# Product keys: two of every four weighings move from VectorE to GpSimd; the row-length count of two attentions goes through column tiles

## The chip, the cores and the metric

One core of one Trainium2 chip runs the whole program, a stack of four transformer layers in float32. The time is device microseconds (us) of one launch. The engines are PE (TensorE, matrix products), DVE (VectorE), ACT (ScalarE), POOL (GpSimd) and SP (which issues the transfers). Each runs its own list of instructions in order and waits on semaphores for the others.

## The reference

x has 16 batches of 128 tokens with 128 features. The change touches the third layer only (two attentions and a feed-forward with product keys):

```python
def self_attn(x, Wq, Wk, Wv):                       # cross_attn: the same without causal
    Q, K, V = (x @ Wq, x @ Wk, x @ Wv)
    energy = jnp.einsum('bqd,bkd->bqk', Q, K)
    lengths = jnp.sum(energy[:, 0] != 0, axis=-1)    # from the first query's row
    pad = kidx[None, None, :] >= lengths[:, None, None]
    energy = jnp.where(pad | causal, NEG_INF, energy)
    score = jax.nn.softmax(energy / np.sqrt(DK), axis=-1)
    return jnp.einsum('bqk,bkd->bqd', score, V)
...
def _L2_ffn_ref(x, w_q, keys, expert_down, expert_up, norm_w):   # H=8 heads, K=8, 32x32 experts
    sim1, sim2 = ...                                 # 32 similarities for either half of a key
    s1, i1 = top_k(sim1, K); s2, i2 = top_k(sim2, K)
    fs, pk = top_k(s1[..., :, None] + s2[..., None, :], K)
    hidden = gelu(einsum('btd,bthkd->bthk', xn, expert_down[fi])) * relu(fs)
    return einsum('bthk,bthkd->btd', hidden, expert_up[fi])
```

The kernel does not gather experts. It computes gelu(xn @ down) for all 1024 experts of each token, builds for each token a 32x32 table of given weights (the sum over heads of the scores that were chosen, zero elsewhere), multiplies the two element by element ("weighs") and projects out.

## The kernel before, in words

**Two attentions** (`two_attentions`). The 16 batches form four groups ("chunks", c = 0 to 3) of four. A list of stages (`ATTEND`), each one step later for each next group, gives one common order, `ORDER`, from which every engine takes its own instructions. Per group and attention: PE makes q, k (stage "project") and v ("values"), then in stage "scores" the scores, the causal part, and the counts: for each batch the product of all keys with the first query, 128 rows by 1 column. DVE turns these into 0 and 1 (`count`). Stage "length": PE adds them up over the rows with a column of ones, DVE copies the four lengths and makes a 4x128 row of large negative numbers (`measure_length`). Stage "mask": PE spreads it over the scores with four products. Then DVE takes row maxima ("top"), ACT the exponentials ("exp"), PE turns them ("flip"), ACT stores that, PE multiplies with v ("pv"), and layer norm and turning follow.

**Product keys** (`product_keys`). One round i for each batch i, and four rounds more to drain. In a round:

- PE: two chunks of the hidden layer of the next group of four (`hide`), the similarities of batch i+2 (`score`), the table of given weights of batch i-1 (`give`, 32 small products into the PSUM tile `given_ps`), and after the last batch of a group the projection (`project_out`, 128 products) and its turning (`finish`).
- DVE: maxima of the similarities of batch i (`tops`, 16 instructions), comparison against them (`parts`), the eighth best pair sum (`threshold`), the choice (`compare`, two instructions), the weighing of batch i-2 (`weigh`, hidden times `given_ps`, which it reads straight from PSUM), and two transposes of the factors (`turn`: right, then left).
- POOL: pair sums (two short ones), two sums of 512 elements into `factors`, and for the right and then the left side a subtraction and a product (`split_made`, `cut_made`), which `turn` waits for.
- ACT: a copy of half the similarities (`store_half`, which `tops` waits for), two gelus, and four copies that spread the turned right factor into `blocks` (`spread`, needs the right transpose and `given_made` of the batch before). `give` needs `blocks`, the left transpose, and the weighing of the batch before, since there is only one `given_ps`.

Of the kernel before, what the change touches and what calls it, by code (L numbers as in the profile page):

```python
# [15 lines left out]
P = 128  # L16
# [2074 lines left out]
def two_attentions(nc, m, w, tag, meanwhile, fold_of, keys_ahead, values_ahead):  # L2091
# [4 lines left out]
    ATTEND = ("project", "values", "scores", "length", "mask", "top", "exp", "flip", "pv", "stats", "scale", "turn")  # L2096
# [4 lines left out]
    with cleared_semaphores(nc) as new_semaphore, ExitStack() as ctx:  # L2101
# [12 lines left out]
        def room(n):  # L2114
# [10 lines left out]
        nonzero, length = chunk("nonzero", [P, 4]), chunk("length", [4, 1])  # L2125
        neg = chunk("neg", [4, S], BF16)
# [16 lines left out]
        nonzero_made, length_made, neg_made, neg_max_made = [  # L2143
            [sem(f"{n}{c}") for c in range(NCH)] for n in ("nonzero_made", "length_made", "neg_made", "neg_max_made")]
# [49 lines left out]
        def _(pe):  # L2194
# [22 lines left out]
            for name, a, c in ORDER:  # L2217
# [14 lines left out]
                elif name == "scores":  # L2232
                    work.wait_freed(pe, ("q", a, c), 0)
                    if not a:
                        work.wait_freed(pe, ("k", a, c), 0)
                    scores.wait_free(pe, (a, c), 0)
# [5 lines left out]
                    counts.wait_free(pe, (a, c), 0)  # L2242
                    for q in range(4):
                        ins = mm(counts.bank((a, c))[:, 0, q:q + 1], keys[a][c][:, q, :], qT[c][:, q, 0:1], start=True, stop=True)
                    counts.fill(ins, (a, c))
                elif name == "length":
                    pe.wait_ge(nonzero_made[c], a + 1)
                    mm(counts.bank((a, c))[0:4, 1, 0:1], nonzero[c][:, :], m["ones_sq"][:, 0:1],
                       start=True, stop=True).then_inc(length_made[c], 1)
                elif name == "mask":  # L2250
                    pe.wait_ge(neg_made[c], a + 1)
                    bank = scores.bank((a, c))
                    for q in range(4):
                        ins = mm(bank[:, q, :], m["pick_bf"][0:4, q, :], neg[c][:, :], start=False, stop=(q == 3))
                    scores.fill(ins, (a, c))
# [69 lines left out]
        def _(dve):  # L2325
# [3 lines left out]
            def count(a, c):  # L2329
                counts.wait_filled(dve, (a, c), 0)  # L2330
                V.tensor_scalar(nonzero[c][:, :], counts.bank((a, c))[:, 0, 0:4], 0.0, None, ALU.not_equal) \
                    .then_inc(nonzero_made[c], 1)

            def measure_length(a, c):
                dve.wait_ge(length_made[c], a + 1)
# [69 lines left out]
def product_keys(nc, m, w, tag, meanwhile):  # L2405
# [5 lines left out]
    with cleared_semaphores(nc) as new_semaphore, ExitStack() as ctx:  # L2411
# [81 lines left out]

        def exists(b):
            return 0 <= b < B

        @block.sync
        def _(sp):
            meanwhile(sp)
# [556 lines left out]
```

## Time and profile before

| | |
|---|---|
| runs, median (lowest to highest of 3) | 1214.05 us (1205.83 to 1220.04) |
| the profiled execution: its time | 1209.49 us |
| its span, first to last instruction | 1207.6 us |
| mean granted TensorE clock | 0.887 of full |
| PE, DVE, ACT, POOL busy over the span | 970.9, 744.0, 576.3, 391.7 us |
| the two attentions, 742.5 to 841 us of the span | 98.5 us |
| product keys, 841 to 1058.4 us | 217.4 us |

All positions below are microseconds from the start of the span. The busy shares over the whole span say little about either stage: they are an average over eight layers with different limits.

### The profile page before, as it was taken

The numbers are of one execution on the slowest core, as the hardware profiler recorded it, in microseconds if no ns is written. First come the engines' busy times: TensorE is split into PE (matmuls) and PEld (weight loads), VectorE is DVE, ScalarE is ACT, GpSimd is POOL, SyncE is SP. The second block draws the span as 40 slices with busy tenths as digits, with TensorE's granted clock in tenths as the row PEclk, the third lists the DMA queues.
The fourth block names the chain that finished last, engine by engine and source line by source line (L and its number), as shares of the span: only waits on it lengthen the run. The fifth ranks groups of instructions, "written<-read, shape, count | busy, mean of one in ns | idle before, by whom it ended". The sixth has DMA issues, their size and how long they took to land. (4 is left out here: it accounts for less than half of the span.)

```text
span 1207.6 us, 26748 instructions
## 1 busy us (share of the span) xinstructions
PE 970.9 (80%) x10817; PEld 642.7 (53%) x10845; DVE 744.0 (62%) x2025; ACT 576.3 (48%) x945; POOL 391.7 (32%) x418
## 2 busy tenths in 40 slices
PE   4999799998999977988897763785657577489987
PEld 2677333433333424776675562563456466447766
DVE  3586666546655464653574134468899999557752
ACT  3465465644555425644652631665535354235531
POOL 4320200000000022775002665146576656333340
PEclk9899799998999988998896886987878788789987
DMA  6000000000000016000000322000000000000000
GB/s 268 2 2 2 19 1 1 0 1 0 1 0 1 0 41 240 2 4 2 2 3 12 96 68 92 1 1 1 2 2 3 1 3 3 2 1 2 2 2 36
DMA packets 14713, 27.77 MB, mean 23 GB/s; under 512 B 1024, under 2 KB 12416, under 8 KB 13696
## 3 DMA queue, kind: packets, MB, share of 16 engines
q1 hardware_dynamic: 13568, 23.97, 5.5%
q0 software_dynamic: 1024, 2.10, 0.6%
q8 instruction: 87, 1.43, 0.5%
q14 instruction: 34, 0.28, 0.1%
HBM read 20.17 MB, written 5.90 MB: 22 GB/s over the span
## 5 line engine op out<-in xcount | busy, mean ns | idle before, releaser
L1324 PE MATMUL l0f_ctl<-l1f_in,l0f_in 128*128 128x512 f32 x320 | 145.7, 598 | 0.5
L548 DVE TENSOR_REDUCE l_neg_max<-l_ring 128x4 f32<-128x512 f32 x128 | 82.1, 684 | 63.5 <-PE l_ring L410 62.9
L128 POOL TENSOR_SCALAR row_var_eps<-row_mean_var 128x12 f32<-128x12 f32 (+2 forms) x16 | 3.7, 230 | 362.5 <-DVE row_mean_var L123 361.8
L2600 ACT COPY l2f_blocks_sb<-l2f_right_t_sb 32x1024 f32<-32x1024 f32 x64 | 66.8, 1043 | 86.6 <-PE l2f_given_ps L2531 75.5
L507 ACT ACTIVATE l_probs<-l_scores 128x1024 f32<-128x1024 f32 x64 | 65.6, 1025 | 82.2 <-PE l_scores L418 82.2
L1324 PEld LDWEIGHTS l0f_ctl<-l1f_in,l0f_in 128*128 128x128 f32 x320 | 61.7, 193 | 71.4 <-issue 70.2
L2531 PE MATMUL l2f_given_ps<-l2f_blocks_sb,l2f_left_t_sb 128*32 128x128 f32 x1024 | 50.1, 376 | 40.1 <-DVE l2f_hid_sb L2700 35.6
L2531 PEld LDWEIGHTS l2f_given_ps<-l2f_blocks_sb,l2f_left_t_sb 128*32 128x32 f32 x1024 | 44.0, 153 | 54.0 <-issue 53.8
L698 POOL TENSOR_TENSOR l_squares<-l_exps 128x1024 f32<-128x1024 f32 x32 | 60.6, 1895 | 29.8 <-ACT l_exps L953 29.8
L1045 DVE TENSOR_REDUCE l_neg_max<-l_scores 128x8 f32<-128x1024 f32 x32 | 39.2, 1225 | 43.4 <-PE l_scores L750 43.4
L368 POOL TENSOR_SCALAR_AFFINE_SELECT l_probs<-l_probs 128x1024 f32<-128x1024 f32 x32 | 35.0, 1094 | 64.0 <-ACT l_probs L507 64.0
L1597 DVE TENSOR_SCALAR l0f_halt<-l0f_halt 128x512 f32<-128x512 f32 x8 | 3.4, 427 | 78.8 <-ACT l0f_halt L1483 78.8
L1590 DVE SCALAR_TENSOR_TENSOR l1f_in<-l0f_index,l0f_in,l0f_hidden 128x512 f32<-128x512 bf16 x64 | 43.5, 747 | 12.2 <-ACT l0f_index L1464 11.0
L2664 POOL TENSOR_TENSOR l2f_factors_sb<-l2f_factors_sb,l1f_in 128x512 f32<-128x512 f32 x32 | 48.1, 1503 | 0.0
L953 ACT ACTIVATE l_exps<-l_scores 128x1024 f32<-128x1024 f32 x32 | 32.8, 1025 | 30.0 <-PE l_scores L756 29.8
L1324 PE MATMUL l0f_work<-xnT,l0f_in 128*128 128x512 f32 (+2 forms) x88 | 45.0, 683 | 1.3 <-ACT xnT L204 0.7
L750 PE MATMUL l_scores<-l_k_heads,l_q_all 32*128 32x256 f32 x256 | 36.8, 402 | 10.0 <-DVE l_neg_max L1045 8.3
L410 PE MATMUL l_ring<-l_k_heads,l_q_all 32*128 32x256 f32 x256 | 39.1, 424 | 6.5 <-ACT l_probs L507 2.4
L2509 PE MATMUL l2f_sim_ps<-l1f_in,xnT 128*128 128x512 f32 x32 | 22.5, 792 | 27.1 <-DVE l1f_in L2690 27.1
L1446 ACT ACTIVATE l0f_hidden<-l0f_work,l0f_in 128x512 f32<-128x512 f32 (+1 forms) x40 | 27.3, 686 | 29.0 <-PE l0f_work L1324 28.9
L992 ACT ACTIVATE l_exps<-l_scores 128x1024 f32<-128x1024 f32 x32 | 31.0, 1021 | 20.7 <-PE l_scores L837 20.7
L756 PE MATMUL l_scores<-l_q_all,l_k_heads 32*128 32x128 f32 x512 | 37.7, 286 | 1.8 <-ACT l_exps L953 1.8
(466 smaller groups left out, 2635.2 us busy)
## 6 DMA issues: line engine op xcount, KB each, us to landing
l1f_in<-in_l1f SPq DMA_DIRECT2D x1, 4580.0 KB, 13.5
l0f_in<-in_l0f SPq DMA_DIRECT2D x1, 2302.5 KB, 8.4
l1f_in<-in_l2u SPq DMA_DIRECT2D x1, 2048.0 KB, 8.7
sorted_rows<-first_in SPq DMA_DIRECT2D x1, 1856.0 KB, 10.4
l0f_in<-in_l2f SPq DMA_DIRECT2D x1, 1792.5 KB, 18.0
l1f_sorted<-sorted_rows SPq DMA_DIRECT2D x7, 256.0 KB, 4.9
expert_rows<-l1f_sorted SPq DMA_DIRECT2D x7, 256.0 KB, 2.2
x_in<-in_x SPq DMA_DIRECT2D x1, 1024.0 KB, 4.9
```

Of the source, the lines that this page charges most:

```text
L410: ins1 = mm(score_bank(b, half, g)[:, :, t, :], q_all[r, b, t, :], k_heads[r, b, t, :, :], start=not causal, stop=True, skip_group_check=True)
L507: nc.scalar.activation(probs[c % 2][:, 2 * pair:2 * pair + 2], scores2[:, :, :, :, :], ACT.Exp, scale=SCORE_SCALE).then_inc(exp_done, 1)
L548: ring.free(V.tensor_reduce(out, score_bank(b, half, g), AX.X, ALU.max, negate=True), ("score", b, half, g))
L698: nc.gpsimd.tensor_tensor(squares[c % 2][:, pair], e, e, ALU.mult).then_inc(squared, 1)
L750: ins1 = mm(scores1[:, g, :, t, :], q_all[r, b, t, :], k_heads[r, b, t, :, :], start=True, stop=True, skip_group_check=True)
L756: ins2 = mm(scores2[:, g, j, t, :], k_heads[r, c, t, j, :], q_all[r, c, t, :], start=True, stop=True, skip_group_check=True)
L1045: V.tensor_reduce(out, scores1[:, :, :, :, :].rearrange("p g j t s -> p (g j) t s"), AX.X, ALU.max, negate=True).then_inc(max_taken, 1)
L1324: return nc.tensor.matmul(out, lhs, rhs, start=start, stop=stop)
L1590: ins = STT(chosen[c % 2][:, k, p, :], index[k][:, c % 2, :], w["row_expert"][:, p:p + 1], hidden[c % 2][:, p, :], ALU.is_equal, ALU.mult)
L2531: ins = mm(given_ps[K * j:K * j + K, s, :, :], left_t[b % 2][:, 8 * j + s, :], blocks[:, 8 * j + s, :, :], start=True, stop=True)
L2600: A.copy(blocks[rows, :, u, :], right_t[rows, :, :]).then_inc(blocks_made, 1)
L2664: TT(value, value, kept[:, side, :, :], ALU.mult).then_inc(cut_made, 1)
```

## The change

**Product keys.** Of each four batches DVE weighs the first and the last, and POOL the second and third (`ON_POOL = (1, 2)`). POOL has no access to PSUM, so ACT first copies `given_ps` (128x1024) into `given_sb` (`store_given`, ahead of `spread` in the round), and `give` of the next batch waits for that copy and not for the weighing. POOL weighs at the end of its round and reads `given_sb` with its inner step over s, 128 elements apart. On DVE, the maxima of the next batch (`tops(i + 1)`) now stand ahead of the transposes of this one.

**Attentions.** The counts come first in stage "scores" and the other way round: the first 32 queries as weights and the keys as the moving side, so that batch q of the group writes rows 32q to 32q+31 of one PSUM tile, 128 columns wide. DVE compares with zero (128x128), sums along the row and makes a 128x512 mask that is -1 (never masked) outside each batch's own first row. PE adds that mask with one product. Stage "length" is gone, so "mask" and all behind it stand one step earlier in `ORDER`. Two constants move to the input group `l2f`, which grows by 288 KB, and one of 128 KB leaves the common group.

```diff
-    ATTEND = ("project", "values", "scores", "length", "mask", "top", "exp", "flip", "pv", "stats", "scale", "turn")
+    ATTEND = ("project", "values", "scores", "mask", "top", "exp", "flip", "pv", "stats", "scale", "turn")
...
+                    counts.wait_free(pe, (a, c), 0)
+                    for q in range(4):
+                        ins = mm(counts.bank((a, c))[32 * q:32 * q + 32, 0, :], qT[c][:, q, 0:32], keys[a][c][:, q, :],
+                                 start=True, stop=True)
+                    counts.fill(ins, (a, c))
                     scores.wait_free(pe, (a, c), 0)
...
-                    for q in range(4):
-                        ins = mm(counts.bank((a, c))[:, 0, q:q + 1], keys[a][c][:, q, :], qT[c][:, q, 0:1], start=True, stop=True)
-                    counts.fill(ins, (a, c))
-                elif name == "length":
-                    pe.wait_ge(nonzero_made[c], a + 1)
-                    mm(counts.bank((a, c))[0:4, 1, 0:1], nonzero[c][:, :], m["ones_sq"][:, 0:1],
-                       start=True, stop=True).then_inc(length_made[c], 1)
                 elif name == "mask":
                     pe.wait_ge(neg_made[c], a + 1)
-                    bank = scores.bank((a, c))
-                    for q in range(4):
-                        ins = mm(bank[:, q, :], m["pick_bf"][0:4, q, :], neg[c][:, :], start=False, stop=(q == 3))
-                    scores.fill(ins, (a, c))
+                    scores.fill(mm(scores.bank((a, c))[:, :, :], fold_of["first_rows_bf"][:, :], neg[c][:, :, :],
+                                   start=False, stop=True), (a, c))
...
+            def mask_beyond_length(a, c):
                 counts.wait_filled(dve, (a, c), 0)
+                counts.free(V.tensor_scalar(nonzero[c][:, :], counts.bank((a, c))[:, 0, :], 0.0, None, ALU.not_equal), (a, c))
                 counts.wait_freed(dve, (a, c), 0)
+                own(V.tensor_reduce(length[c][:, :], nonzero[c][:, :], AX.X, ALU.add))
+                V.tensor_scalar(neg[c][:, :, :], fold_of["key_of_row"][:, :, :], length[c][:, 0:1], NEG, ALU.is_ge, ALU.mult) \
                     .then_inc(neg_made[c], 1)
...
+    ON_POOL = (1, 2)
...
             def give(b):
                 pe.wait_ge(left_turned, b + 1)
                 pe.wait_ge(blocks_made, 4 * b + 4)
-                if b:
-                    pe.wait_ge(weighted, b)
+                if b and on_pool(b - 1):
+                    pe.wait_ge(given_stored, count(b, True))
+                elif b:
+                    pe.wait_ge(weighted, count(b, False))
...
+            def store_given(b):
+                act.wait_ge(given_made, b + 1)
+                if count(b, True):
+                    act.wait_ge(weighted_pool, count(b, True))
+                A.copy(given_sb[:, :, :, :], given_ps[:, :, :, :]).then_inc(given_stored, 1)
...
+                if exists(i - 2) and on_pool(i - 2):
+                    store_given(i - 2)
                 if exists(i):
                     spread(i)
...
+            def weigh(b):
+                g, q = b // GB, b % GB
+                if q == ON_POOL[0]:
+                    gelu_done(pool, b)
+                pool.wait_ge(given_stored, count(b + 1, True))
+                hidden = hid[g % 2][:, :, q, :].rearrange("p k (u s) -> p k u s", u=4)
+                TT(hidden, hidden, given_sb.rearrange("p s u k -> p k u s"), ALU.mult).then_inc(weighted_pool, 1)
...
+                if exists(b - 2) and on_pool(b - 2):
+                    weigh(b - 2)
+            weigh(B - 2)
...
             norm.dve(dve)
+            tops(0)
             for i in ROUNDS:
                 if exists(i):
-                    tops(i)
                     parts(i)
-                if exists(i):
                     threshold(i)
                     compare(i)
-                if exists(i - 2):
+                if exists(i - 2) and not on_pool(i - 2):
                     weigh(i - 2)
+                if exists(i + 1):
+                    tops(i + 1)
                 if exists(i):
                     turn(i)
```

DVE in product keys, one round before the change. MAX of 16 is `tops`, MAX of 8 `threshold`, the two TENSOR_TENSOR of 512 into `l1f_in` are `compare` (its tiles are carved from the space of `l1f_in`), the one on `l2f_hid_sb` is `weigh`:

```order
L2676 MAX l1f_in<-l2f_sim_ps 128x8 x16
L2686 TENSOR_TENSOR l2f_factors_sb<-l2f_sim_ps,l1f_in 128x8x64 x2
L2690 SCALAR_TENSOR_TENSOR l1f_in<-l2f_factors_sb,l2f_sim_ps 128x256
L2707 MAX l1f_in<-l1f_in 128x8 x8
L2715 TENSOR_TENSOR l1f_in<-l2f_factors_sb,l1f_in 128x512 x2
L2700 TENSOR_TENSOR l2f_hid_sb<-l2f_hid_sb,l2f_given_ps 128x32x32
L2723 STREAM_TRANSPOSE l2f_right_t_sb<-l2f_factors_sb 128x32x32
L2729 STREAM_TRANSPOSE l2f_left_t_sb<-l2f_factors_sb 128x32x32
```

The same place on DVE after the change, from `parts` of a round without a weighing to `tops` in the middle of it and the transposes:

```order
L2708 TENSOR_TENSOR l2f_factors_sb<-l2f_sim_ps,l1f_in 128x8x64 x2
L2712 SCALAR_TENSOR_TENSOR l1f_in<-l2f_factors_sb,l2f_sim_ps 128x256
L2728 MAX l1f_in<-l1f_in 128x8 x8
L2736 TENSOR_TENSOR l1f_in<-l2f_factors_sb,l1f_in 128x512 x2
L2698 MAX l1f_in<-l2f_sim_ps 128x8 x16
L2744 STREAM_TRANSPOSE l2f_right_t_sb<-l2f_factors_sb 128x32x32
L2750 STREAM_TRANSPOSE l2f_left_t_sb<-l2f_factors_sb 128x32x32
```

The weighing is gone from this round, and the 16 maxima stand where it stood, for the next batch.

POOL in the same rounds after the change (L2654 is the weighing, the only row that is new; the rest is a whole round of before between two weighings):

```order
L2654 TENSOR_TENSOR l2f_hid_sb<-l2f_hid_sb,l1f_in 128x32x32
L2663 TENSOR_TENSOR l1f_in<-l1f_in 128x8x16
L2666 TENSOR_TENSOR l1f_in<-l1f_in 128x8x12
L2672 TENSOR_TENSOR l2f_factors_sb<-l1f_in 128x8x64
L2675 TENSOR_TENSOR l2f_factors_sb<-l1f_in 128x8x64
L2680 TENSOR_TENSOR l2f_factors_sb<-l2f_factors_sb 128x8x32
L2683 TENSOR_TENSOR l2f_factors_sb<-l2f_factors_sb,l1f_in 128x8x64
L2680 TENSOR_TENSOR l2f_factors_sb<-l2f_factors_sb 128x8x32
L2683 TENSOR_TENSOR l2f_factors_sb<-l2f_factors_sb,l1f_in 128x8x64
L2654 TENSOR_TENSOR l2f_hid_sb<-l2f_hid_sb,l1f_in 128x32x32
```

The weighing ends POOL's round, so all that POOL does for the next batch stands behind it.

PE in the first attention before the change, one step of the order (L2201 the projections or, of 128x128, the values; L2239 scores; L2241 the causal part; L2244 counts; L2248 length; L2254 mask):

```order
L2201 MATMUL l_work<-xnT,l_in 128x512 x2
L2254 MATMUL l_scores<-l_neg_sb,common_in 128x128 x4
L2248 MATMUL l_counts<-common_in,l_nonzero_sb 4x1
L2239 MATMUL l_scores<-l_kT_sb,l_qT_sb 128x128 x4
L2241 MATMUL l_scores<-common_in 128x512
L2244 MATMUL l_counts<-l_qT_sb,l_kT_sb 128x1 x4
L2201 MATMUL l_work<-l_in,xnT 128x128 x4
```

The same step after it:

```order
L2200 MATMUL l_work<-xnT,l_in 128x512 x2
L2248 MATMUL l_scores<-l_neg_sb,l0f_in 128x512
L2237 MATMUL l_counts<-l_kT_sb,l_qT_sb 32x128 x4
L2243 MATMUL l_scores<-l_kT_sb,l_qT_sb 128x128 x4
L2245 MATMUL l_scores<-common_in 128x512
L2200 MATMUL l_work<-l_in,xnT 128x128 x4
```

The counts stand ahead of the scores, the length is gone, and the mask here is that of group 1 where before it was that of group 0.

## Rows read from the trace of the kernel before

**Rows 1.** Busy time of each engine in two stretches: attentions, then product keys.

```profile
core 0: us, PE busy (x) PEld busy (x) DVE busy (x) ACT busy (x) POOL busy (x), PEclk, DMA share, GB/s
742.50:841.00 98.50, 72.80 (x450) 54.69 (x452) 61.20 (x269) 57.62 (x157) 42.17 (x51) 0.86 0.06 22
841.00:1058.40 217.40, 142.12 (x3136) 117.37 (x3136) 194.94 (x561) 97.88 (x136) 128.68 (x136) 0.80 0.01 2
```

**Rows 2.** Timeline of DVE, one round of product keys: start, us, what.

```profile
908.92 1.29 DVE L2686 TENSOR_TENSOR l2f_factors_sb<-l2f_sim_ps,l1f_in 128x512 f32<-128x512 f32 x2
...
910.58 0.87 DVE L2707 MAX8 l1f_in<-l1f_in 128x8 f32<-128x36 f32 x8
911.49 1.99 DVE L2715 TENSOR_TENSOR l1f_in<-l2f_factors_sb,l1f_in 128x512 f32<-128x512 f32 x2
913.40 1.21 DVE L2700 TENSOR_TENSOR l2f_hid_sb<-l2f_hid_sb,l2f_given_ps 128x1024 f32<-128x1024 f32 x1
914.70 2.19 DVE L2723 STREAM_TRANSPOSE l2f_right_t_sb<-l2f_factors_sb 128x1024 f32<-128x1024 f32 x1
916.76 2.09 DVE L2729 STREAM_TRANSPOSE l2f_left_t_sb<-l2f_factors_sb 128x1024 f32<-128x1024 f32 x1
918.72 1.67 DVE L2676 MAX8 l1f_in<-l2f_sim_ps 128x8 f32<-128x32 f32 x16
920.41 1.29 DVE L2686 TENSOR_TENSOR l2f_factors_sb<-l2f_sim_ps,l1f_in 128x512 f32<-128x512 f32 x2
```

**Rows 3.** Timeline of DVE, first round: idle before it, and releaser, in brackets.

```profile
857.21 2.08 DVE L2723 STREAM_TRANSPOSE l2f_right_t_sb<-l2f_factors_sb 128x1024 f32<-128x1024 f32 x1 [1.25 <-POOL l2f_factors_sb L2664]
```

**Rows 4.** Timeline of POOL in the round of rows 2.

```profile
909.65 1.06 POOL L2653 TENSOR_TENSOR l2f_factors_sb<-l1f_in 128x512 f32<-128x512 f32 x1
910.75 1.06 POOL L2656 TENSOR_TENSOR l2f_factors_sb<-l1f_in 128x512 f32<-128x512 f32 x1
911.76 1.17 POOL L2661 TENSOR_TENSOR l2f_factors_sb<-l2f_factors_sb 128x256 f32<-128x256 f32 x1
912.89 1.71 POOL L2664 TENSOR_TENSOR l2f_factors_sb<-l2f_factors_sb,l1f_in 128x512 f32<-128x512 f32 x1
...
915.25 1.29 POOL L2664 TENSOR_TENSOR l2f_factors_sb<-l2f_factors_sb,l1f_in 128x512 f32<-128x512 f32 x1
```

**Rows 5.** Groups of instructions of 128x1024: busy, mean ns, idle before.

```profile
L507 ACT ACTIVATE l_probs<-l_scores 128x1024 f32<-128x1024 f32 x64 | 65.6, 1025 | 82.2 <-PE l_scores L418 82.2
L698 POOL TENSOR_TENSOR l_squares<-l_exps 128x1024 f32<-128x1024 f32 x32 | 60.6, 1895 | 29.8 <-ACT l_exps L953 29.8
```

**Rows 6.** Timeline at the end of product keys, ACT and PE.

```profile
1037.16 4.24 ACT L2600 COPY l2f_blocks_sb<-l2f_right_t_sb 32x1024 f32<-32x1024 f32 x4 [8.78 <-PE l2f_given_ps L2531]
...
1041.51 3.39 PE L2531 MATMUL l2f_given_ps<-l2f_blocks_sb,l2f_left_t_sb 128*32 128x128 f32 x64 [4.45 <-ACT l2f_blocks_sb L2600]
```

**Rows 7.** Timeline of PE in the first attention.

```profile
759.83 0.95 PE L2244 MATMUL l_counts<-l_qT_sb,l_kT_sb 128*128 128x1 f32 x8
760.64 1.14 PE L2201 MATMUL l_work<-l_in,xnT 128*128 128x128 f32 x8
...
764.86 0.39 PE L2254 MATMUL l_scores<-l_neg_sb,common_in 4*128 4x128 bf16 x4
765.18 0.19 PE L2248 MATMUL l_counts<-common_in,l_nonzero_sb 128*4 128x1 f32 x2
765.30 1.16 PE L2239 MATMUL l_scores<-l_kT_sb,l_qT_sb 128*128 128x128 f32 x8
```

**Rows 8.** Timeline of PE in product keys: products in column tiles.

```profile
926.06 1.95 PE L2520 MATMUL l2f_work_ps<-xnT,l0f_in 128*32 128x128 f32 x64 [0.34 <-ACT l1f_in L2608]
```

**Rows 9.** Timeline of ACT and DVE at the first exponentials of each attention.

```profile
768.50 0.59 ACT L2286 COPY l_v_sb<-l_work 128x512 f32<-128x512 f32 x1 [2.95 <-PE l_work L2201]
770.40 0.37 ACT L2301 ACTIVATE l_qT_sb<-l_scores,l_neg_max_sb 128x128 f32<-128x128 f32 x1
...
797.35 0.16 DVE L2331 TENSOR_SCALAR l_nonzero_sb<-l_counts 128x4 f32<-128x4 f32 x1 [1.42 <-PE l_counts L2244]
798.35 0.37 ACT L2301 ACTIVATE l_qT_sb<-l_scores,l_neg_max_sb 128x128 f32<-128x128 f32 x1 [2.74 <-DVE l_neg_max_sb L2344]
```

More of the change, by code:

```diff
@@ L2124, in two_attentions @@
         res = [[rows[:, 4 * c:4 * c + 4, :] for c in range(NCH)], room(0), room(1)]
-        nonzero, length = chunk("nonzero", [P, 4]), chunk("length", [4, 1])
-        neg = chunk("neg", [4, S], BF16)
+        nonzero, length = [room(1)[c][:, 0, :] for c in range(NCH)], chunk("length", [P, 1])
+        neg = chunk("neg", Q4, BF16)
         raw_max, neg_max = chunk("raw_max", [P, 4]), chunk("neg_max", [P, 4])
@@ L2142, in two_attentions @@
                        [sem("counts_filled")], [sem("counts_freed")])
-        nonzero_made, length_made, neg_made, neg_max_made = [
-            [sem(f"{n}{c}") for c in range(NCH)] for n in ("nonzero_made", "length_made", "neg_made", "neg_max_made")]
+        neg_made, neg_max_made = [[sem(f"{n}{c}") for c in range(NCH)] for n in ("neg_made", "neg_max_made")]
         eps_added, rstd_made, normed, res_made = [
@@ L2389, in _ @@
                 if name == "scores":
-                    count(a, c)
-                elif name == "length":
-                    measure_length(a, c)
+                    mask_beyond_length(a, c)
                 elif name == "top":
@@ L2495, in exists, with on_pool, count, gelu_done @@
             return 0 <= b < B
+        def on_pool(b):
+            return b % GB in ON_POOL
+        def count(b, pool):
+            return sum(on_pool(c) == pool for c in range(b))
+        def gelu_done(eng, b):
+            for c in range(KK - WORK, KK):
+                wait_freed(eng, ("hid", b // GB, c))
         @block.sync
@@ L2537, in project_out @@
                     wait_free(pe, ("out", g, j))
-                pe.wait_ge(weighted, GB * g + GB)
+                pe.wait_ge(weighted, count(GB * g + GB, False))
+                pe.wait_ge(weighted_pool, count(GB * g + GB, True))
                 for k in range(K):
@@ L2695, in weigh @@
                 if q == 0:
-                    for c in range(KK - WORK, KK):
-                        wait_freed(dve, ("hid", g, c))
+                    gelu_done(dve, b)
                 dve.wait_ge(given_made, b + 1)
```

18 lines of the change are left out of this document (7 added, 11 removed).

## The prediction

> **What bounds the kernel now.** The change lives in two stages, so I read the trace by stage first. In product keys DVE is busy 194.9 of 217.4 us, the others 60% or less [rows 1]; in the attentions no engine passes 75%, so order and latency set the time there and PE is merely the fullest.
>
> Then one round of product keys on DVE, by starts [rows 2]. From one `parts` (908.92) to the next (920.41) it takes 11.49 us: parts 1.66, threshold 0.91, compare 1.91, weigh 1.30, right transpose 2.06, left 1.96, maxima 1.69. There is no gap in it: what leaves DVE shortens the round, until another chain ends later. The nearest one is POOL's [rows 4]. Counted from the start of parts, its right product ends at 912.89 + 1.71 = 5.68 us and its left one at 915.25 + 1.29 = 7.62 us, and the two transposes start at 5.78 and 7.84. POOL is 0.1 us from being the bound. In the first round, which has nothing to weigh yet, it is: DVE stands idle for 1.25 us ahead of the right transpose, released by POOL's product [rows 3]; the second round, also without a weighing, looks the same. Taking the weighing away alone would thus turn 1.2 of its 1.3 us into a wait.
>
> **Product keys, DVE.** With the maxima of the next batch between compare and the transposes, the right transpose of a round without a weighing starts at 1.66 + 0.91 + 1.91 + 1.69 = 6.17 us (POOL is ready at 5.68), the left one at 8.23 (ready at 7.62), and the round ends at 10.19 instead of 11.49. POOL's chain hangs on `parts`, not on where the maxima stand, so its 5.68 and 7.62 hold: its second sum started at 1.83, behind parts, and does so still. The rounds that lose DVE's weighing and lie on the path are i = 3, 4, 7, 8, 11, 12 and 15 (batches 1, 2, 5, 6, 9, 10, 13; batch 14 falls in the drain). Six give 1.30 us each, 7.8. Round 15 has no maxima behind it and runs into POOL's 5.68 again: 0.1. Rounds 0 and 1 lose their wait: 2 x 1.2 = 2.4. Against this, rounds 8 and 12 follow a projection, for which PE holds back `give`, hence ACT's spreading and the copy that the maxima need, and the maxima now want it 3.5 to 4.8 us earlier in the round; following the chain with the durations of these rows I find some 0.5 us of wait in either, 1.1 together. Sum: 7.8 + 0.1 + 2.4 - 1.1 = 9.2 us. In the rounds with a weighing nothing is gained: their DVE work stays 11.49.
>
> **ACT's new copy.** Eight of 128x1024 from PSUM; the nearest row is 1.03 us [rows 5]. ACT is busy 97.9 of 217 us [rows 1], and the copy stands ahead of the spreading. What is queued behind it is the spreading of this round, which waits for the right transpose anyway, so seven of the eight lie in idle time. The last does not: behind the spreading of batch 15 (1037.16, 4.24 us) ACT now copies the table of batch 14 before the last `give` (1041.51) can start [rows 6]: +1.0. But the 8.78 us for which ACT waited there went on the `give` that DVE's weighing of batch 13 held up; it is now held by a copy that is done much earlier, and the spreading can start at the end of the right transpose, an estimated 1.7 us sooner. I book the end at 0 (bounds -0.7 and +1.0).
>
> **POOL's weighing, the unknown.** No row shows POOL on 1024 elements with a far inner step. Without the step: 1.9 us [rows 5], or twice 1.06 to 1.29 for 512, 2.1 to 2.6 [rows 4]; beside DVE's compare, which reads two SBUF tensors too, 512 took 1.71 and 256 took 1.17, hence 3.4 and 4.7. It starts at 7.62 and runs beside DVE's maxima and transposes, where the rows read 1.29, so I take 2.6. It ends at 10.2, the two short pair sums end 0.73 later at 10.95, and the next round's first sum of 1.06 ends at 12.0 = 10.19 + 1.8, just when the second sum could start. It costs nothing up to about 3.2 us, since the transposes leave another 0.5. From there I let each step of the two chains start at the later of its predecessors, round by round: 3.6 us leaves 7.9 of the 9.2 to 9.5, 4.4 leaves 4.7, 5.2 nothing, 6.5 makes it 10.6 us slower. Rounds behind an `add` or with a weighing on DVE absorb part of the delay, which is why the loss starts gently. For contention with two engines busier I take 0.2 off: 9.0 us.
>
> The Trainium skill speaks against my 2.6. "GPSIMD Engine Reference", section 7 (Performance pitfalls for Q7 kernels), says that a GpSimd read of SBUF whose step times element size is over 8 bytes costs about 50% more per element. Here the inner step of the given table is 128 elements. By it 2.6 would be 3.9 us, and the stage would give 6.7 instead of 9.0. No row of this trace shows such a read on POOL.
>
> **Attentions.** From the counts to the next product took PE 760.64 - 759.83 = 0.81 us, the length 765.30 - 765.18 = 0.12, the mask 0.32 [rows 7]. In column tiles 64 passes of 128 columns take 1.95 us [rows 8], so the eight of the new counts take 0.25. The one mask product writes the same 512 columns as the four: I take the same 0.32 (not below 0.2). Per group 0.56 + 0.12 = 0.68 us leave PE. In the first attention PE runs nearly without a gap up to the values of group 3; ACT stores these at 768.50, loads a table, and starts the first exponential at 770.40 [rows 9]. Ahead of them stand three counts and two lengths less, and one mask more: 1.7 + 0.2 - 0.3 = 1.6 us, which shift all that follows. In the second, the first exponential (798.35) waited 2.74 us for DVE, whose maxima stood behind the count of group 2 (797.35). Without the length stage they stand behind that of group 1, about 3.3 us earlier. Then the turning of the first probabilities is next, on PE behind the scores of group 3, with four counts and three to four lengths less ahead: 2.3 us after small waits. Together 3.9. The bounds are 1.5 (the waits eat the second) and 6. DVE's part grows from three short ones (0.57) to a compare of 128, a sum and a mask of 512, by estimate 1.0 us a group: between counts and mask PE has scores and a projection or values, over 2 us, and DVE is idle there. The 288 KB in the input load lie in a transfer that has a whole layer of cover; removed 128 KB at the start I count at nothing.
>
> **Sum.** 9.0 + 3.9 = 12.9 us. The profiled execution took 1209.49 us with a span of 1207.6, so its like would be 1196.6. It is 4.6 us under the median of the runs; against the median of 1214.05 I predict **1201 us**. A measurement of this kernel tells about 1% (12 us) from no change, and the forecast lies right at that edge.
>
> **Rivals.**
>
> 1. *The strided read costs POOL.* Weighing of 3.6 to 4.4 us, from the rows of 2.6 and the contended 4.7. Speaks for it: the inner step, and the rule above. Against: POOL's other reads here with hops between runs of 32 are not slow. Stage gain 4.7 to 7.9, total 10: 1204. Chance 0.2.
> 2. *The attentions give nothing*: the mask waits for DVE's longer work, or layer norm behind them is bound by DVE anyway. Total 9: 1205. Chance 0.1.
> 3. *POOL becomes the bound.* Strided and contended together: 3.4 us times 1.5 to 2, 5.1 to 6.8. `threshold` then waits for the pair sums and both transposes for the products, in all seven rounds; slower than before from 5.2 us in the stage and about 5.8 in the kernel; at 6.5, 10.6 - 3.9 = +6.7: 1221. Chance 0.05.
> 4. *More than summed*, as PE, with less to do, passes the slow stretches faster and the attentions give 6: total 16, 1198. Chance 0.1.
>
> **How the numbers follow.** The forecast has 0.55; its own spread (10.5 to 15) lies more than half beyond 12 us. Faster by over 1%: 0.34 of it, 0.08 of rival 4, 0.06 of 1 and 2 (the median of before is itself loose, 1206 to 1220), and 0.02 else: 0.50. Slower by over 1%: 0.03. The rest, 0.47, is within. Range: 1191 (a gain of 16 on a median 7 lower) to 1210.
>
> **What would show it.** In the profile after: rounds of product keys of 10.2 and 11.5 us by turns in pairs; POOL's weighing near 2.6 us, ending before the next parts start; no idle ahead of the right transposes but in round 15; on PE counts of 0.25 us and a first exponential 1.6, then 3.9 us earlier. I am wrong if the weighing takes over 3.3 us, if DVE waits for the copy of similarities, or if the mask product waits for DVE.

## The result, and the profile after

The changed kernel takes 1196.43 us (median of 20 runs, 1192.27 to 1207.09), the kernel before 1209.42 (20 runs, 1204.48 to 1220.04): a ratio of 0.9894, 95% interval 0.9874 to 0.9914, 13.0 us less. In a second session the ratio was 0.9869 [0.9837, 0.9901]. The forecast of 1201 us hung on a median of 1214.05 for the kernel before, of three runs; over twenty it is 1209.42, and the 4.6 us between them are the 4.6 by which 1201 was too high. Both ratios say a little over 1% faster, and both intervals reach to just under 1%: that the gain exceeds 1% is likely, not settled. The page of the profiled execution begins:

```profile
span 1191.8 us, 26693 instructions
...
PE 957.7 (80%) x10775; PEld 629.2 (53%) x10805; DVE 740.1 (62%) x2017; ACT 583.4 (49%) x953; POOL 414.4 (35%) x426
```

Where the time went is read by stage, from the first row of the layer norm on DVE in one stage to the first in the next:

| us | before | after | predicted |
|---|---|---|---|
| two attentions | 98.63 | 94.26 | -3.9 |
| product keys | 217.29 | 207.29 | -9.0 |
| all else, by the spans | 891.68 | 890.25 | 0 |

The last line is of layers that the change doesn't touch (more on it under the whole runs, below). The first two are of one execution each; in the others with the same code product keys took 206.8 to 207.0 us, and the attentions 94.2 or 95.4 (point 7 of the account of the prediction). The windows of the two stages answer to [rows 1]: DVE is busy 185.05 us in place of 194.94 in product keys, POOL 151.14 in place of 128.68.

```profile
core 0: us, PE busy (x) PEld busy (x) DVE busy (x) ACT busy (x) POOL busy (x), PEclk, DMA share, GB/s
742.70:836.90 94.20, 65.72 (x408) 45.48 (x412) 67.25 (x269) 57.68 (x157) 42.34 (x52) 0.90 0.06 23
836.90:1044.20 207.30, 136.59 (x3136) 113.22 (x3136) 185.05 (x553) 105.36 (x144) 151.14 (x145) 0.82 0.01 2
```

A round of product keys without a weighing on DVE, and the start of the next, which has one (compare [rows 2]; columns are start, us, engine, what):

```profile
889.63 1.29 DVE L2708 TENSOR_TENSOR l2f_factors_sb<-l2f_sim_ps,l1f_in 128x512 f32<-128x512 f32 x2
...
892.20 1.99 DVE L2736 TENSOR_TENSOR l1f_in<-l2f_factors_sb,l1f_in 128x512 f32<-128x512 f32 x2
894.12 1.65 DVE L2698 MAX8 l1f_in<-l2f_sim_ps 128x8 f32<-128x32 f32 x16
895.69 2.15 DVE L2744 STREAM_TRANSPOSE l2f_right_t_sb<-l2f_factors_sb 128x1024 f32<-128x1024 f32 x1
897.68 2.24 DVE L2750 STREAM_TRANSPOSE l2f_left_t_sb<-l2f_factors_sb 128x1024 f32<-128x1024 f32 x1
900.05 1.29 DVE L2708 TENSOR_TENSOR l2f_factors_sb<-l2f_sim_ps,l1f_in 128x512 f32<-128x512 f32 x2
...
902.62 1.99 DVE L2736 TENSOR_TENSOR l1f_in<-l2f_factors_sb,l1f_in 128x512 f32<-128x512 f32 x2
904.53 1.21 DVE L2721 TENSOR_TENSOR l2f_hid_sb<-l2f_hid_sb,l2f_given_ps 128x1024 f32<-128x1024 f32 x1
905.66 1.65 DVE L2698 MAX8 l1f_in<-l2f_sim_ps 128x8 f32<-128x32 f32 x16
```

From parts to parts it is 900.05 - 889.63 = 10.42 us, no idle in it. Behind the first maxima of the stage, the one wait for the copy of half the similarities is in round 7:

```profile
927.84 1.67 DVE L2698 MAX8 l1f_in<-l2f_sim_ps 128x8 f32<-128x32 f32 x16 [0.38 <-ACT l1f_in L2593]
```

POOL's weighing and ACT's copy of the table, as groups (count, then busy and mean ns, then the idle before):

```profile
L2654 POOL TENSOR_TENSOR l2f_hid_sb<-l2f_hid_sb,l1f_in 128x1024 f32<-128x1024 f32 x8 | 23.1, 2893 | 2.8 <-ACT l1f_in L2609 2.8
L2609 ACT COPY l1f_in<-l2f_given_ps 128x1024 f32<-128x1024 f32 x8 | 8.2, 1026 | 0.1
```

The last round and the drain on DVE: the right transpose waits again [rows 3], the last weighing waits for PE's `give`.

```profile
1019.28 2.08 DVE L2744 STREAM_TRANSPOSE l2f_right_t_sb<-l2f_factors_sb 128x1024 f32<-128x1024 f32 x1 [1.23 <-issue]
...
1030.52 1.22 DVE L2721 TENSOR_TENSOR l2f_hid_sb<-l2f_hid_sb,l2f_given_ps 128x1024 f32<-128x1024 f32 x1 [5.29 <-PE l2f_given_ps L2533]
```

In the first attention PE now goes from mask to counts to scores in 0.31 + 0.35 us (compare [rows 7]), and the first exponentials of the two attentions on ACT start 26.26 and 51.11 us after the stage's start, in place of 27.86 and 55.81 [rows 9]:

```profile
764.06 0.38 PE L2248 MATMUL l_scores<-l_neg_sb,l0f_in 128*128 128x512 bf16 x1
764.37 0.43 PE L2237 MATMUL l_counts<-l_kT_sb,l_qT_sb 128*32 128x128 f32 x8
764.72 1.16 PE L2243 MATMUL l_scores<-l_kT_sb,l_qT_sb 128*128 128x128 f32 x8
```

```profile
768.92 0.37 ACT L2295 ACTIVATE l_qT_sb<-l_scores,l_neg_max_sb 128x128 f32<-128x128 f32 x1
...
793.77 0.37 ACT L2295 ACTIVATE l_qT_sb<-l_scores,l_neg_max_sb 128x128 f32<-128x128 f32 x1
```

### The profile page after: what moved, and what is told of

Read it like the earlier page. It is cut to its first block and busy times, and to the rows that moved or that the text cites. A ratio compares the mean times of both kernels' runs of the same rounds, so it can differ in the third digit from the quotient of the medians.

```text
span 1191.8 us, 26693 instructions
## 1 busy us (share of the span) xinstructions
PE 957.7 (80%) x10775; PEld 629.2 (53%) x10805; DVE 740.1 (62%) x2017; ACT 583.4 (49%) x953; POOL 414.4 (35%) x426
## 2 busy tenths in 40 slices
DMA packets 14713, 27.94 MB, mean 23 GB/s; under 512 B 1024, under 2 KB 12416, under 8 KB 13696
## 3 DMA queue, kind: packets, MB, share of 16 engines
q0 software_dynamic: 1024, 2.10, 0.6%
```

## The experiments

Stage times below are read as in the table above. The kernels are named by what they are.

**One half of the change alone: `attn_only` and `keys_only`.** The changed kernel with `product_keys` of before, and the kernel before with `product_keys` of the changed one.

> The attentions of the changed kernel with the product keys of before. My theory (PE loses 0.68 us a group in the first attention, and in the second DVE's maxima stand one group earlier): the attentions end 3.9 us sooner (bounds 1.5 and 6), product keys take their old 217.3 us; against before -3.9 us, ratio 0.997. The rival that the attentions give nothing expects 0. A third reading, that the whole gain of 13 us has its source here, expects -13.

> The product keys of the changed kernel with the attentions of before. My theory: -9 to -10 us against before (ratio 0.992), all of it between the first normalising row of the layer and the first of the next, which goes from 217.3 to about 207.3 us. If the two parts help each other (the clock, for example) this and the attentions alone sum to less than 13; if they are independent, to 13 to 14.

| | attentions | product keys | run, median | ratio to before |
|---|---|---|---|---|
| attn_only | 94.22 | 217.25 | 1205.24 | 0.9957 [0.9929, 0.9986] |
| keys_only | 98.63 | 206.76 | 1206.59 | 0.9969 [0.9942, 0.9997] |

Each half works in its own stage, 4.4 and 10.5 us (in the whole kernel 4.4 and 10.0), and gives nothing in the other: the two parts don't interact inside the stages. The runs of `keys_only`, though, fell by 3.9 us only. That was taken up again (last experiment).

**The two moves in product keys apart: `maxima_only` and `weigh_only`**, both with the attentions of the changed kernel.

```diff
 # maxima_only: maxima ahead of the turns, all sixteen weighings on DVE
-    ON_POOL = (1, 2)
+    ON_POOL = ()
```

```diff
 # weigh_only: weighings split, each batch's maxima ahead of its own parts as before
-            tops(0)
...
+                    tops(i)
                     parts(i)
...
-                if exists(i + 1):
-                    tops(i + 1)
```

> The changed kernel, but DVE weighs all batches again; the next maxima stay ahead of the transposes. My theory: only the waits of rounds 0 and 1 go, 1.2 us each, so product keys take 217.3 - 2.4 = 214.9 us, and all later rounds 11.49 us. The rival that POOL's chain is shortened in every round by the early maxima expects rounds below 11.49 us.

> The changed kernel, but the maxima stand at the head of each round as before; POOL weighs two of four. My theory: in the rounds without a weighing DVE waits some 1.2 us for POOL's product ahead of the right transpose, so that seven weighings of 1.3 us buy about 0.1 us each: product keys take 216.3 us (-1). The rival that the DVE work removed is what counts (the order of the maxima being a detail) expects 217.3 - 9.1 = 208.2 us.

`weigh_only`: 217.36 us for the stage, no gain at all, where 1.0 us was expected. A round whose weighing had moved to POOL, on DVE:

```profile
891.54 1.99 DVE L2736 TENSOR_TENSOR l1f_in<-l2f_factors_sb,l1f_in 128x512 f32<-128x512 f32 x2
894.75 2.23 DVE L2744 STREAM_TRANSPOSE l2f_right_t_sb<-l2f_factors_sb 128x1024 f32<-128x1024 f32 x1 [1.23 <-issue]
896.89 2.06 DVE L2750 STREAM_TRANSPOSE l2f_left_t_sb<-l2f_factors_sb 128x1024 f32<-128x1024 f32 x1
898.86 1.22 DVE L2698 MAX8 l1f_in<-l2f_sim_ps 128x8 f32<-128x32 f32 x12
```

Between compare, which ends at 891.54 + 1.99, and the right transpose stand 1.2 us of idle in place of the weighing. The releaser is given as issue, but POOL's right product ended just before, at 892.94 + 1.72 = 894.66, and the gap is that of [rows 3] to 0.03 us. The 1.30 us that the weighing left are taken by POOL's chain, as worked out from [rows 4].

`maxima_only`: 213.68 us, 3.6 less, where 2.4 was expected. Its first round, with the maxima in the gap:

```profile
852.76 2.00 DVE L2734 TENSOR_TENSOR l1f_in<-l2f_factors_sb,l1f_in 128x512 f32<-128x512 f32 x2
854.69 1.65 DVE L2696 MAX8 l1f_in<-l2f_sim_ps 128x8 f32<-128x32 f32 x16
856.26 2.04 DVE L2742 STREAM_TRANSPOSE l2f_right_t_sb<-l2f_factors_sb 128x1024 f32<-128x1024 f32 x1
858.22 1.96 DVE L2748 STREAM_TRANSPOSE l2f_left_t_sb<-l2f_factors_sb 128x1024 f32<-128x1024 f32 x1
860.31 1.29 DVE L2706 TENSOR_TENSOR l2f_factors_sb<-l2f_sim_ps,l1f_in 128x512 f32<-128x512 f32 x2
```

No idle is left; the first two rounds are 1.24 and 1.21 us shorter than before. The other 1.2 us come from the later rounds, which take between 0.13 us more and 0.33 us less than before, half of it in rounds 7 and 11 (0.33 and 0.30); points 1 and 3 below show how the same instructions start sooner or later by their neighbours. So the moves are worth 3.6 and 0 us alone and 10.0 together: the weighing pays only once the maxima fill the gap.

**What the step in POOL's read costs: `dense_table`.**

```diff
-        given_sb = carve([8, 4, K])
+        given_sb = carve([K, 4, 8])
...
-                A.copy(given_sb[:, :, :, :], given_ps[:, :, :, :])
+                A.copy(given_sb.rearrange("p k u s -> p s u k"), given_ps[:, :, :, :])
...
-                TT(hidden, hidden, given_sb.rearrange("p s u k -> p k u s"), ALU.mult)
+                TT(hidden, hidden, given_sb[:, :, :, :], ALU.mult)
```

> The changed kernel with one thing other: ACT writes the given table into SBUF in the order in which POOL reads it, so that POOL's weighing reads runs without a gap in place of an inner step of 128 elements; ACT's copy now writes in short hops. The step is what it costs (rival 1 of the prediction, in a milder form): the weighing falls from the 2.90 us of the changed kernel to 2.1 to 2.6. The step costs nothing: it stays at 2.9. ACT's copy: 1.03 us or somewhat more. Either way the stage takes the 207.3 us of the changed kernel within 0.5, since POOL's chain has slack at 2.9 us.

```profile
L2654 POOL TENSOR_TENSOR l2f_hid_sb<-l2f_hid_sb,l1f_in 128x1024 f32<-128x1024 f32 x8 | 19.1, 2386 | 4.4 <-ACT l1f_in L2609 4.4
L2609 ACT COPY l1f_in<-l2f_given_ps 128x1024 f32<-128x1024 f32 x8 | 15.5, 1940 | 0.1
```

POOL falls from 2.89 to 2.39 us, ACT's copy grows from 1.03 to 1.94. The step was in POOL's price, 0.50 us or 21%, and moving it to ACT costs 0.91 there. The stage took 207.43 us. Both are slack in the rounds; the drain, where the copy stands in the chain, grew from 30.71 (after the last parts) to 31.65.

**How much slack POOL has: `pool_plus_512` and `pool_twice`.** Ahead of each of the eight weighings POOL does more work into a table that nothing reads (`spent` makes the engine wait for the end of each such instruction).

```diff
 # pool_plus_512
+                spent(TT(unused[:, :, :, :], given_sb[:, 0:4], given_sb[:, 4:8], ALU.mult))
                 TT(hidden, hidden, given_sb.rearrange("p s u k -> p k u s"), ALU.mult).then_inc(weighted_pool, 1)
```

```diff
 # pool_twice
+                for half in range(2):
+                    spent(TT(unused.rearrange("p s u k -> p k u s"), hidden[:, :, :, 0:4],
+                             given_sb[:, 4 * half:4 * half + 4].rearrange("p s u k -> p k u s"), ALU.mult))
```

> The changed kernel with one more product of 512 elements (contiguous, into a table that nothing reads) on POOL ahead of each of the eight weighings, so that POOL's work per weighing grows from 2.90 us to 4.1 to 4.4. The prediction's two chains then give a stage 3.5 to 5 us longer than the changed kernel's 207.3: 210.8 to 212.3, with DVE idle ahead of the threshold or the right transpose of the round behind each weighing. Rival: POOL's slack is larger than the 0.5 us that the prediction gave it, and the stage stays at 207.3 to 208.5.

> The changed kernel with POOL's strided product done once more (in two halves, into a table that nothing reads) ahead of each of the eight weighings: 5.8 to 6.2 us per weighing, the case of the prediction's rival 3. The two chains give a stage that is slower than that of the kernel before (217.3): 5 to 8 us slower, 222 to 225, or 15 to 18 above the changed kernel's 207.3. Rival: rounds with no weighing on POOL absorb more than the chains say, and the stage ends at 212 to 217.

With 1.28 us more per weighing the stage took 211.65 us, within what the two chains say. DVE now stands still for POOL ahead of the threshold and ahead of compare:

```profile
887.36 0.88 DVE L2732 MAX8 l1f_in<-l1f_in 128x8 f32<-128x36 f32 x8 [0.34 <-POOL l1f_in L2670]
888.45 2.61 DVE L2740 TENSOR_TENSOR l1f_in<-l2f_factors_sb,l1f_in 128x512 f32<-128x512 f32 x2 [0.21 <-POOL l2f_factors_sb L2676]
...
899.03 0.88 DVE L2732 MAX8 l1f_in<-l1f_in 128x8 f32<-128x36 f32 x8 [0.38 <-POOL l1f_in L2670]
900.11 2.58 DVE L2740 TENSOR_TENSOR l1f_in<-l2f_factors_sb,l1f_in 128x512 f32<-128x512 f32 x2 [0.21 <-POOL l2f_factors_sb L2676]
```

The waits are 0.34 and 0.21 us in the first such round, 0.38 and 0.21 in the next, and compare takes 2.6 us in place of 1.99. Four rounds (4, 5, 9 and 13) are 1.2 to 1.3 us longer for it. In the changed kernel the pair sums end 0.9 us ahead of the threshold (890.37 and 891.29 in the round shown above), and POOL's right product 0.35 ahead of its transpose. Yet the transposes don't wait here, since the threshold and compare, which come first, have been put off already. With 3.1 us more (two of 1.555) the stage took 226.70 us, 9.4 slower than the kernel before, and beyond the upper end of the expectation by 1.7:

```profile
892.91 0.88 DVE L2734 MAX8 l1f_in<-l1f_in 128x8 f32<-128x36 f32 x8 [2.36 <-POOL l1f_in L2672]
...
906.40 0.88 DVE L2734 MAX8 l1f_in<-l1f_in 128x8 f32<-128x36 f32 x8 [2.56 <-POOL l1f_in L2672]
```

Rival 3 of the prediction is thus real at a weighing of 6 us, twice the one that came, through the threshold; the transposes don't wait here either. The rounds account for 5.4 of the 9.4 us (181.60 against 176.20 in the kernel before, first to last parts). The drain gives the other 4.0, and is where more came than was expected: it took 34.89 us, in the changed kernel 30.71. ACT's last copy waits 1.56 us for POOL; the projection then waits 1.1 us longer for POOL's weighing of batch 14; and it takes 9.05 us in place of 7.43, at a granted clock of 0.81 in place of 1.00.

**Where ACT's copy is hidden: `copy_twice`.**

```diff
+                for half in range(2):
+                    spent(A.copy(unused[:, :, :, :], given_ps[:, 4 * half:4 * half + 4, :, :]))
                 A.copy(given_sb[:, :, :, :], given_ps[:, :, :, :]).then_inc(given_stored, 1)
```

> The changed kernel with ACT's copy of the given table done once more (in two halves, into a table that nothing reads) ahead of each of the eight copies: some 1.2 us more of ACT in eight rounds. By the prediction seven of the eight lie in idle time of ACT, and only the last stands in the chain of the drain: the stage grows by 1 to 2 us, from 207.3 to 208.3 to 209.3. Rival: the copies hold up PE's next give, and through it the weighing of the next batch on DVE: up to 8 x 1.2, a stage of 212 to 217.

From the first parts to the last it took 165.65 us, 166.38 in the changed kernel: 1.2 us more on ACT in each of six rounds between them cost nothing. The seventh copy lies in the last round, behind the last parts. The drain took 34.18 us in place of 30.71:

```profile
1020.73 4.25 ACT L2606 COPY l2f_blocks_sb<-l2f_right_t_sb 32x1024 f32<-32x1024 f32 x4 [3.90 <-PE l2f_given_ps L2535]
...
1025.00 1.20 ACT L2613 COPY l1f_in<-l2f_given_ps 128x512 f32<-128x512 f32 x2
1026.23 1.01 ACT L2614 COPY l1f_in<-l2f_given_ps 128x1024 f32<-128x1024 f32 x1
...
1027.39 3.64 PE L2535 MATMUL l2f_given_ps<-l2f_blocks_sb,l2f_left_t_sb 128*32 128x128 f32 x64 [6.78 <-ACT l1f_in L2614]
...
1032.56 9.17 PE L2547 MATMUL l2f_work_ps<-l2f_hid_sb,l1f_in 32*128 32x128 f32 x256 [1.53 <-DVE l2f_hid_sb L2726]
```

The last `give` starts 15.09 us after the last parts (1012.30), 13.32 in the changed kernel (1026.82 - 1013.50): 1.77 us of the 3.5 are the copies. The eighth gives 1.24. The seventh gives 0.53: it makes the `give` before late, and ACT's spreading, which now waits for that, starts 8.43 us after the last parts in place of 7.90. In the changed kernel this `give` ended 0.8 us ahead of the spreading, so there the seventh copy is hidden, by less than its own length. The other 1.7 is the projection, 9.17 us in place of 7.43, at a granted clock of 0.80 in place of 1.00. The stage, 210.02, lies 0.7 above the expectation, and would lie within it without that.

**The last copy alone: `last_on_dve`.**

```diff
-            return b % GB in ON_POOL
+            return b % GB in ON_POOL and b != B - 2
```

> The changed kernel with batch 14, whose weighing falls in the drain, weighed by DVE from PSUM again, so that no copy on ACT stands behind the spreading of batch 15 (the prediction's +1.0 at the end). If that copy is in the chain that ends the stage, product keys take 206.2 to 206.5 us in place of 207.3. Rival: the last give waits for the left transpose or PE anyway, and the stage stays at 207.1 to 207.5.

The stage took 206.17 us, just what the theory said, but the rows say it was for another reason. The drain fell by 0.35 us only, 30.36:

```profile
1018.33 4.25 ACT L2603 COPY l2f_blocks_sb<-l2f_right_t_sb 32x1024 f32<-32x1024 f32 x4 [4.61 <-DVE l2f_right_t_sb L2743]
...
1022.06 1.19 DVE L2720 TENSOR_TENSOR l2f_hid_sb<-l2f_hid_sb,l2f_given_ps 128x1024 f32<-128x1024 f32 x1
...
1023.39 3.64 PE L2533 MATMUL l2f_given_ps<-l2f_blocks_sb,l2f_left_t_sb 128*32 128x128 f32 x64 [5.88 <-DVE l2f_hid_sb L2720]
```

The last `give` starts 12.95 us after the last parts (1010.44), 0.37 earlier. The copy is gone, but DVE's weighing of batch 14 stands behind the left transpose and ends at 1023.25, 0.7 after ACT's spreading: it takes most of the copy's place. The other 0.8 us the edit does not touch: 0.45 lie ahead of the first parts (9.75 us in place of 10.20), where TensorE was granted 0.73 of its clock instead of 0.52, and 0.32 in the rounds (166.06 in place of 166.38). In all thirteen other executions the first parts started 10.19 to 10.22 us after the stage. That the total hit the expectation is luck.

**Order or PE's time in the attentions: `stage_kept`.**

```diff
-ATTEND = ("project", "values", "scores", "mask"
+ATTEND = ("project", "values", "scores", "empty", "mask"
```

> The changed kernel with an empty stage where the length stage stood, so that each mask, maximum and all that follows stand one step later in the order again, with the shorter work on PE as changed. By the prediction the first attention gains through PE's time alone and the second through the order: the first exponential of the first attention starts as in the changed kernel, that of the second some 2 to 3 us later, and the two attentions take 96 to 97.5 us in place of 94.3. Rival: PE's shorter work alone makes the gain, and they take 94.3 to 95.4.

The attentions took 94.46 us: the rival. The rows are the first exponential of the second attention on ACT and the turning of its result on PE, then the same turning in the changed kernel:

```profile
792.15 0.37 ACT L2295 ACTIVATE l_qT_sb<-l_scores,l_neg_max_sb 128x128 f32<-128x128 f32 x1 [1.99 <-DVE l_neg_max_sb L2334]
...
793.72 0.66 PE L2206 MATMUL l_work<-first_in,l_qT_sb 128*128 128x128 f32 x4 [0.64 <-ACT l_qT_sb L2295]
```

```profile
796.66 0.60 PE L2206 MATMUL l_work<-first_in,l_qT_sb 128*128 128x128 f32 x4
```

The exponential starts 52.63 us after the stage's start, 1.5 later than in the changed kernel, so the order does move it. But the turning starts at 54.20 and 54.00 us (before: 57.47). PE reaches it no sooner in either order, since the scores of group 3 stand ahead. So the gain is not the order of the stages but what this kernel keeps of the change: PE's shorter work, and the counts ahead of the scores, a move that no run takes apart from it. The earlier maximum only leaves its exponentials waiting for PE.

**The whole runs: `after_again` and `keys_again`.** Two programs once more, with no edit.

> The changed kernel once more, to see what a second execution of the same program repeats. Theory: the stages that the change touches repeat (attentions 94.3 to 95.4 us, product keys 207.3 within 0.5), while the first attention layers, which it does not touch and which took 117.3 and 189.8 us, move by up to 4 us between executions with the stretches at half clock; the ratio to the kernel before is 0.987 to 0.992. Rival: the untouched layers repeat to 0.3 us, so that what they take belongs to each built program, and a change of the code moves them.

> The kernel before with the product keys of the changed one, once more. In its first execution the stage took 206.8 us in place of 217.3, yet the ratio of the runs was 0.997, 3.9 us where 9 to 10 were expected. Theory: that was the scatter of the runs, and the ratio now is 0.990 to 0.994 (7 to 12 us less), with a stage of 206.8 within 0.5. Rival: something of this mixed kernel gives back 5 us outside the stage in the runs that are not profiled, and the ratio is 0.996 to 0.998 again.

| | attentions | product keys | second layer's attention | fourth layer's attention | run, median | ratio |
|---|---|---|---|---|---|---|
| after | 94.26 | 207.29 | 189.96 | 113.09 | 1196.43 | 0.9894 [0.9874, 0.9914] |
| after_again | 95.45 | 206.90 | 185.86 | 113.91 | 1193.93 | 0.9869 [0.9837, 0.9901] |
| keys_only | 98.63 | 206.76 | 189.93 | 113.76 | 1206.59 | 0.9969 [0.9942, 0.9997] |
| keys_again | 98.66 | 206.78 | 193.21 | 124.03 | 1200.75 | 0.9933 [0.9905, 0.9961] |

Product keys repeat to 0.4 us in one program and to 0.02 in the other, and the ratio of keys alone is now within what the theory said (0.990 to 0.994). Layers that neither edit touches move by 4 us between two executions of one program, in one case by 10. The clock tells it: the first 40 us of the fourth layer's attention in `keys_again`, then in `keys_only` (TensorE's granted clock is the third number from the end):

```profile
1050.00:1090.00 40.00, 37.59 (x268) 20.52 (x268) 19.89 (x38) 12.71 (x18) 11.66 (x17) 0.62 0.00 1
```

```profile
1049.00:1089.00 40.00, 36.55 (x395) 23.19 (x396) 22.37 (x50) 17.23 (x26) 15.45 (x21) 0.91 0.01 1
```

Granted 0.62 in place of 0.91, PE does 268 products where it did 395. TensorE has two levels there, 1.2 and 2.4 GHz, a window shows the mix, and the stretches at the lower one fall differently in each execution. So the runs of one program spread by 15 us, and the stage is a sharper measure of an edit than the run is.

By the medians keys alone gained 6.5 us in the second session (1200.75 against 1207.21; its ratio would be 8.1), in both sessions together 4.6 (1205.0 of 24 runs, 1209.6 of before's), where the stage gives 10.5. The first ratio's interval doesn't hold the stage's gain, the second's does. Beside the changed attentions the same edit gives 9 (1196.4 against 1205.2). Whether the mixed kernel meets more stretches at half clock elsewhere, as its profiled 124.03 would suggest, stays open: it is one execution.

## Why the prediction was right

It said 12.9 us less; it was 13.0 by the medians and 14.4 in the two stages (13.6 in `after_again`). Point by point:

1. *Rounds that lose the weighing: 6 x 1.30 less 1.1 of waits, 6.7.* Measured, by starts of parts in rounds 3, 4, 7, 8, 11 and 12: 0.98, 1.10, 1.01, 1.06, 1.31, 1.05, together 6.5. That the total is right is luck: two errors cancel. A round gives 1.1, not 1.30: the left transpose is now followed by parts, which starts 2.13 to 2.37 us after it, where the maxima mostly started after 1.96 (1.89 to 2.08; in rounds 7 and 11, where `add` stands between, 3.8 to 3.9 in both). Parts waits for that transpose's semaphore, the maxima don't; that this is the reason is likely, and no run shows it. And the waits for the half copy of the similarities, booked as two of 0.5 us in rounds 8 and 12, were one of 0.38, in round 7; in `keys_only` there was none.
2. *Rounds 0 and 1, 2.4.* 1.18 and 1.17 (11.36 and 11.54 became 10.18 and 10.37), and `maxima_only` shows that it is the order that does it.
3. *Rounds that keep the weighing: 0.* They gave 0.07 to 0.21 each, 1.0 in seven: a term that was put at nothing, and most of what makes 10.0 of 9.0. The same instructions in another order overlap differently at their seams: maxima start 1.13 us after the weighing, the transpose did after 1.30; it starts 1.57 after the maxima, parts did after 1.69; against both stands the 0.2 to 0.4 of point 1.
4. *Round 15, 0.1.* The idle is there again, 1.23 us, up to 0.1 us after the end of POOL's right product (1017.47 + 1.72); round 15 and the drain together took 30.71 us in place of 30.88.
5. *ACT's copy, 1.03, hidden but at the end.* 1.01 to 1.03, and hidden in six rounds even at twice and more; the seventh is hidden at 1.0 but not at 2.2 (`copy_twice`). At the end the earlier spreading (1.68 us, said 1.7) outweighs the +1.0 a little: the last `give` starts 13.32 us after the last parts in place of 13.93. The rows stand behind this list.
6. *POOL's weighing, 2.6 (1.9 to 4.7), free to 3.2.* It took 2.86 to 2.91. Free, yes: no wait ahead of threshold or compare. The curve behind it was read at two more places: at 4.15 us the chains leave about 5.7 of 9.5, measured 211.65, hence 5.6 of gain; at 6.0 they say 6.5 slower, measured 9.4, of which 5.4 in the rounds and 4.0 in the drain, which the chains took as it was. The Trainium skill's 50% for such a step ("GPSIMD Engine Reference", section 7, Performance pitfalls for Q7 kernels) is right in its sign here, but not in its size: `dense_table` shows 21%, on the whole instruction with one of its two inputs stepped. By the estimate of 3.9 us that was worked out from it the stage would have given 6.7, not 10.0; the measurement decides.
7. *Attentions, 3.9.* 4.4 in this execution. Over eleven with the changed attentions it was 4.2 to 4.4 in four (94.21 to 94.46) and 3.2 to 3.3 in seven (95.35 to 95.45), against 98.63 to 98.66 over three with the old. Of the 1.2 us between the two kinds 1.0 is lost in one stretch, 27 to 33 us into the stage: TensorE was granted 1.00 of its clock there in the first kind and 0.72 in the second, where the product with v takes 2.1 us in place of 1.16 (rows behind this list). The kernel before was granted 1.00 there in all three. So 3.9 lies between two values, and the 4.4 is the larger of them. The counts took 0.35 us, not 0.25: a group of eight in column tiles takes 0.04 each where 64 took 0.03 each. The first exponential came 1.60 earlier, as said, but by two errors again: counts, lengths and mask give 1.2 of it, and the rest is 0.1 in each of five places where the same products follow one another sooner (the row of the values lasts 1.05 us where it lasted 1.14). The turning in the second attention came 3.5 earlier, said 3.9. The mask waited for DVE once, 0.17 us. The order of the maxima, with which the prediction explained the second attention, gives 0.2 us (`stage_kept`); what carried the gain is its other term, the work on PE ahead of the turning.

The drain in the changed kernel, ACT and PE (compare [rows 6]):

```profile
1021.40 4.25 ACT L2603 COPY l2f_blocks_sb<-l2f_right_t_sb 32x1024 f32<-32x1024 f32 x4 [4.58 <-DVE l2f_right_t_sb L2744]
...
1025.67 1.01 ACT L2609 COPY l1f_in<-l2f_given_ps 128x1024 f32<-128x1024 f32 x1
...
1026.82 3.64 PE L2533 MATMUL l2f_given_ps<-l2f_blocks_sb,l2f_left_t_sb 128*32 128x128 f32 x64 [6.22 <-ACT l1f_in L2609]
```

The spreading waited 4.58 us in place of 8.78, and the copy stands between it and `give`.

The product with v in the first attention, in the changed kernel and in its second execution (`after_again`):

```profile
771.81 1.16 PE L2200 MATMUL l_work<-l_v_sb,l_kT_sb 128*128 128x128 f32 x8 [0.46 <-ACT l_kT_sb L2280]
```

```profile
770.25 2.08 PE L2200 MATMUL l_work<-l_v_sb,l_kT_sb 128*128 128x128 f32 x8 [0.46 <-ACT l_kT_sb L2280]
```

Of the rivals, the strided read (1) was half true in mechanism and nothing in time, since 2.9 us still lie under POOL's slack; that the attentions give nothing (2) is refuted by `attn_only`; POOL as the bound (3) didn't come at 2.9 us, cost nearly half the gain at 4.2 and turned it around at 6.0; that much more comes, as the attentions give 6 (4), didn't happen: they gave 3.2 to 4.4, and what product keys gave beyond the sum has the other cause of point 3.

## What to carry to other kernels

Taking work off the fullest engine pays only as far as the next chain behind it: count from the round's start when each partner is ready, and reorder the engine's own work so that its free instructions lie in that gap. Price the moved work on its new engine against that slack, not against zero; here 2.9 us were free, 4.2 cost nearly half the gain and 6 turned it around. When runs scatter by more than the edit, measure the stage, and repeat an execution to see which layers repeat.

## What the runs showed of the hardware

- POOL's product of 1024 elements in SBUF: 2.39 us with both inputs in order, 2.89 with one read at an inner step of 128 elements. ACT's copy of 1024 from PSUM: 1.03 us in order, 1.94 when it writes at an inner step of 32.
- The time from the start of a DVE instruction to the next start depends on what follows: from a left transpose it was 1.89 to 2.08 us in the kernel before, where the maxima of the next batch follow, which wait for nothing recent, and 2.13 to 2.37 in the changed one, where the comparison follows, which waits for the transpose.
- Eight products in column tiles took 0.35 us (0.04 each), 64 took 1.95 (0.03 each).
- The same product with v took 1.16 us in some executions and 2.1 in others, in a stretch of 6 us at a granted clock of 1.00 and 0.72; the two attentions were 1.2 us longer with the second (seven executions of eleven).
- An untouched layer took 113.8 us in one execution and 124.0 in another of the same program, at a granted clock of 0.91 and 0.62 over its first 40 us.
